# A fused attention and mixture-of-experts block: first norm transposed earlier, last gating ahead, residual biases spread over the kernel

## The reference, cut to what matters

```python
x = x + tanh(g_xattn[0]) * xattn(layernorm(x), ctx, ctx)            # 16 heads of 8
x = x + tanh(g_ffn[0]) * ffn(layernorm(x), ...)

def ffn(x, ...):
    attn_out = causal_attention(rope(x), rope(x), x) @ out_proj_w.T + out_proj_b
    x1 = layer_norm(x + attn_out, ln1_w, ln1_b)
    gates = softmax(x1 @ gate_w.T + gate_b)
    _, top_idx = top_k(gates, 2)
    expert_outputs = einsum('bsd,efd->bsef', x1, expert_w) + expert_b
    moe_out = (the two chosen experts' outputs, each times its gate, summed)
    return layer_norm(x1 + moe_out, ln2_w, ln2_b)
```

## Time and profile before

| | us |
|---|---|
| median of 3 runs | 441.61 |
| the profiled execution | 441.23 |
| its span, first to last instruction | 439.4 |
| PE busy | 385.7 (88%) |
| DVE busy | 369.2 (84%) |
| POOL busy | 323.3 (74%) |
| ACT busy | 288.4 (66%) |

### The profile page before, as it was taken

The page is one execution under the profiler, slowest core; times in us unless marked ns, Lnnn a source line. Parts: engine busy times, 40 slices in busy tenths (PEclk is TensorE's granted clock), DMA queues, the critical chain, the costliest instruction groups (busy, mean ns, idle before and its releaser), DMA issues.

```text
span 439.4 us, 17671 instructions
## 1 busy us (share of the span) xinstructions
PE 385.7 (88%) x6538; PEld 231.3 (53%) x6538; DVE 369.2 (84%) x1188; ACT 288.4 (66%) x728; POOL 323.3 (74%) x740
## 2 busy tenths in 40 slices
PE   0368888888888899999999999999999999999994
PEld 0134544454444555666666666666655555555541
DVE  6587999999997878888878878877848999999987
ACT  1126777767766766666666666666665788788772
POOL 4456767767778988888888788849823788888884
PEclk9999999999999999999999999999999999999999
DMA  6855686685553333333434343333000000000001
GB/s 163 193 155 160 170 199 169 162 180 145 132 158 101 98 100 105 104 106 104 109 106 125 103 127 100 99 105 96 12 4 2 1 25 13 24 27 12 25 25 48
DMA packets 88037, 42.76 MB, mean 97 GB/s; under 512 B 16000, under 2 KB 87824, under 8 KB 87952
## 3 DMA queue, kind: packets, MB, share of 16 engines
q1 hardware_dynamic: 80864, 39.59, 34.2%
q10 hardware_dynamic: 7088, 2.04, 2.0%
HBM read 5.69 MB, written 2.10 MB: 18 GB/s over the span
## 4 chain that ended last, share of the span: by engine, by line
PE 41%; DVE 6%; ACT 5%; issue 3%; POOL 1%; SPq 1%; DMA 1%; POOLq 0%; ACTq 0%; DVEq 0%
PE s_bank L923 6%; PE u_bank L499 6%; PE st_bank L923 6%; PE s_bank L421 4%; PE s_bank L434 3%; DVE r L697 2%; PE t_bank L413 2%; PE u_bank L944 2%; PE u_bank L942 2%; PE u_bank L909 2%; PE t_bank L407 2%; ACT z_x_t L1018 2%; ACT part L577 1%; PE u_bank L514 1%; PE t_bank L408 1%
## 5 line engine op out<-in xcount | busy, mean ns | idle before, releaser
L716 DVE TENSOR_REDUCE nm<-s_bank 128x4 f32<-128x512 f32 x256 | 171.5, 683 | 36.3 <-PE s_bank L434 34.0
L599 ACT ACTIVATE pt<-st_bank 128x512 f32<-128x512 f32 x250 | 147.5, 602 | 74.0 <-PE st_bank L434 51.6
L434 PE MATMUL s_bank<-qk 64*64 64x128 bf16 (+1 forms) x1584 | 103.5, 220 | 12.1 <-DVE nm L716 5.7
L499 PE MATMUL u_bank<-pt,vaug 128*32 128x128 f32 x2048 | 108.3, 286 | 1.6 <-DVE ao L733 0.2
L434 PE MATMUL st_bank<-qk 64*64 64x128 bf16 (+1 forms) x1540 | 98.2, 218 | 0.0
L434 PEld LDWEIGHTS s_bank<-qk 64*64 64x64 bf16 (+1 forms) x1584 | 73.8, 104 | 36.1 <-issue 18.9
L434 PEld LDWEIGHTS st_bank<-qk 64*64 64x64 bf16 (+1 forms) x1540 | 69.1, 103 | 0.0
L499 PEld LDWEIGHTS u_bank<-pt,vaug 128*32 128x32 f32 x2048 | 41.1, 108 | 27.5 <-issue 5.2
L421 PE MATMUL s_bank<-mqk,idb 64*64 64x256 bf16 x256 | 38.3, 292 | 0.8 <-ACT pt L599 0.4
L327 POOL TENSOR_TENSOR part<-r,part 128x512 bf16<-128x512 f32 x32 | 37.1, 1158 | 1.4
L421 PE MATMUL st_bank<-mkq,idb 64*64 64x256 bf16 x244 | 35.7, 293 | 0.0
(11 more groups left out here) (136 smaller groups left out, 815.4 us busy)
## 6 DMA issues: line engine op xcount, KB each, us to landing
qk<-part SPq DMA_DIRECT2D x221, 128.0 KB, 2.8
x_all<-x SPq DMA_DIRECT2D x16, 128.0 KB, 2.6
qk<-qrow SPq DMA_DIRECT2D x32, 64.0 KB, 2.0
c_all<-ctx_in SPq DMA_DIRECT2D x14, 128.0 KB, 2.8
out<-z_o SPq DMA_DIRECT2D x14, 128.0 KB, 1.8
qk<-mts ACTq DMA_DIRECT2D x34, 32.0 KB, 2.7
qk<-mts SPq DMA_DIRECT2D x30, 32.0 KB, 2.1
ewt<-exp_t SPq DMA_DIRECT2D x1, 512.0 KB
```

What stands on the lines that cost most here:

```text
L434: ins = pe.matmul(to[outs, :], fixed[:, outs], moving, start=not masked, stop=True, skip_group_check=masked)
L499: ins = pe.matmul(u_bank[b][32 * j:32 * j + 32, r * P:(r + 1) * P], v, pt[m % 4][:, j, :], start=half == 0, stop=half == 1, skip_group_che ...
L599: act.activation(pt[m % 4][:, :, :].rearrange("k j q -> k (j q)"), transposed_bank(m)[:, :], ACT.Exp).then_inc(ex, 1)
L716: dve.tensor_reduce(nm[q % 2][:, first:first + HEADS], s_bank[n % 2][:, :].rearrange("q (j k) -> q j k", j=HEADS), AX_X, ALU.max, negate=T ...
```

## The change

On PE, gated_sum is split: its first product is now sum_of_biases. The order of a full body becomes: experts 4 to 7, transpose of the attention, bias product, transpose of the first norm, gated sum, transpose of the gates, projection, logits, experts 0 to 3. In the body c = 16 the transposes of norm and gates come before the bias product. On ACT, the copy of the norm moves ahead of the second normalisation and of the copy of the gates. The exponentials of the last group's gates go between the two halves of the gating of group 14. On DVE the last group's shift of the logits is issued in body 16 behind the weighing of group 14, and its gating in body 17 ahead of the pair sum of group 14. On POOL the sixteen additions of the bias to the residual are issued one at step 0 of slots 19 to 28 (steps 152, 160, ... 224), one each in steps 242 and 246, and two each at the end of bodies 3 and 4; the two multiplications by tanh(g_ffn) are issued in step 144.

```diff
--- before.py
+++ after.py
@@ -931,7 +931,7 @@
                     pe.wait_ge(norm, SEQS - 1)
                 pe.transpose(u_bank[0][0:G * NE, W:W + P], zg[i][:, :, :].rearrange("q b e -> q (b e)"), idf[:, :]).then_inc(z_gt, 1)
 
-            def gated_sum(g, gc):
+            def sum_of_biases(g, gc):
                 i = gc % 2
                 pe.wait_ge(z_gtc, g + 1)
                 if gc == 0:
@@ -940,6 +940,9 @@
                     pe.wait_ge(z_all, (g - 1) * ALL + 1)
                 dst = u_bank[1][:, 0:W]
                 pe.matmul(dst, zgt[i][:, :], ebs[:, :], start=True, stop=False)
+
+            def gated_sum(g, gc):
+                dst = u_bank[1][:, 0:W]
                 pe.wait_ge(z_yq, g + 1)
                 pe.matmul(dst.rearrange("q (b d) -> q b d", b=G), idf[:, :], zyq[:, :, :],
                           start=False, stop=True).then_inc(z_yb, 1)
@@ -959,14 +962,21 @@
                     experts(s - 2, c - 2, 1)
                 if in_z(c, 0):
                     transpose_att(s, c)
+                if s - 1 == LAST:
+                    transpose_n(s - 1, c - 1)
+                    gates_t(s - 2, c - 2)
+                if in_z(c, 3) and s - 3 < LAST:
+                    sum_of_biases(s - 3, c - 3)
+                if in_z(c, 1) and s - 1 < LAST:
+                    transpose_n(s - 1, c - 1)
+                if s - 2 == LAST:
+                    gates_t(s - 2, c - 2)
                 if in_z(c, 3) and s - 3 < LAST:
                     gated_sum(s - 3, c - 3)
-                if in_z(c, 2):
+                if in_z(c, 2) and s - 2 < LAST - 1:
                     gates_t(s - 2, c - 2)
-                    if s - 2 == LAST:
-                        last_gated_sum(s - 2, c - 2)
-                if in_z(c, 1):
-                    transpose_n(s - 1, c - 1)
+                if s - 2 == LAST:
+                    last_gated_sum(s - 2, c - 2)
                 if in_z(c, 0):
                     project(s, c)
                 if in_z(c, 1):
@@ -1055,6 +1065,8 @@
                 if gc >= 1:
                     act.wait_ge(z_yp, g)
                 for b in range(G):
+                    if b == 1 and g == LAST - 1:
+                        gates_exp(LAST, gc + 1)
                     for e in range(HALF):
                         ins = act.activation(zyg[:, b, e, :], e_bank[b][1][:, e * P:(e + 1) * P], ACT.Copy,
                                              scale=zg[i][:, b, HALF + e:HALF + e + 1])
@@ -1072,22 +1084,25 @@
                     ins.then_inc(z_yg, 1)
 
             def body(s, c):
-                if in_z(c, 2):
+                if in_z(c, 2) and s - 2 < LAST:
                     gates_exp(s - 2, c - 2)
                 if in_z(c, 1):
                     normalise1(s - 1, c - 1)
                 if in_z(c, 0):
                     copy_att(s, c)
+                if in_z(c, 1):
+                    copy_x1(s - 1, c - 1)
+                if s - 1 == LAST:
+                    copy_gates(s - 2, c - 2)
                 if in_z(c, 4) and s - 4 < LAST - 1:
                     normalise2(s - 4, c - 4)
                 if s - 2 == LAST:
                     gate_last_experts(s - 2, c - 2)
-                if in_z(c, 2):
+                if in_z(c, 2) and s - 1 != LAST:
                     copy_gates(s - 2, c - 2)
-                if in_z(c, 1):
-                    copy_x1(s - 1, c - 1)
                 if in_z(c, 2) and s - 2 < LAST:
                     gate_experts(s - 2, c - 2)
+
             def early(n):
                 if n == DRAIN - 9:
                     copy_att(0, 0)
@@ -1260,14 +1275,19 @@
                                              in1=one(x_all, g * G + b), op0=ALU.mult, op1=ALU.add).then_inc(z_yo, 1)
 
             def body(s, c):
-                if in_z(c, 2):
+                if in_z(c, 2) and s - 2 < LAST:
                     shift_logits(s - 2, c - 2)
-                if in_z(c, 3) and s - 3 < LAST:
+                    if in_z(c, 3):
+                        gated_pairs(s - 3, c - 3)
+                    gating(s - 2, c - 2, (s - 3, c - 3) if in_z(c, 3) else None)
+                if s - 2 == LAST:
+                    gating(s - 2, c - 2)
                     gated_pairs(s - 3, c - 3)
-                if in_z(c, 2):
-                    gating(s - 2, c - 2, (s - 3, c - 3) if s - 3 < LAST else None)
+                    gated_sum(s - 3, c - 3)
                 if in_z(c, 2):
                     experts(s - 2, c - 2)
+                if s - 1 == LAST:
+                    shift_logits(s - 1, c - 1)
                 if in_z(c, 0):
                     attention_add(s, c)
                     experts_add(s - 3, c - 3)
@@ -1307,6 +1327,12 @@
             return early, steps
 
         def z_pool(pool):
+            FIRST_BIAS = (GROUPS + 3) * TILES
+
+            def last_bias(g):
+                pool.tensor_tensor(zpair(x_all, g), zpair(x_all, g), l2b[:, :].unsqueeze(1).broadcast_to([P, G, P]),
+                                   ALU.add).then_inc(z_xb, 1)
+
             def x1(g, gc):
                 i = gc % 2
                 pool.wait_ge(z_n, (g + 1) * G)
@@ -1366,16 +1392,20 @@
                     factor1(s, c)
                 if in_z(c, 3) and s - 3 < LAST:
                     factor2(s - 3, c - 3)
+                if c == 3 or c == 4:
+                    last_bias(2 * c + 6)
+                    last_bias(2 * c + 7)
 
             def early(n):
-                if n == DRAIN - 18:
+                if n == FIRST_BIAS - TILES:
                     for t in (l2w, l2b):
                         pool.tensor_scalar(t[:, :], t[:, :], tg[:, 1:2], 0.0, ALU.mult, ALU.add).then_inc(c_l2, 1)
                     pool.wait_ge(c_l2, 2)
-                g = n - DRAIN + 17
-                if 0 <= g < GROUPS:
-                    pool.tensor_tensor(zpair(x_all, g), zpair(x_all, g), l2b[:, :].unsqueeze(1).broadcast_to([P, G, P]),
-                                       ALU.add).then_inc(z_xb, 1)
+                g, t = divmod(n - FIRST_BIAS, TILES)
+                if 0 <= g < 10 and t == 0:
+                    last_bias(g)
+                if g == 11 and t in (2, 6):
+                    last_bias(10 + t // 4)
                 if n == DRAIN - 4:
                     factor1(0, 0)
                 if n == DRAIN - 2:
```

## The result

The changed kernel takes 445.77 us (median of 5 runs, 445.70 to 446.64), the kernel before, in the same comparison, 441.42 us (5 runs, 440.91 to 442.03). The ratio is 1.0102, with a 95% interval of 1.0087 to 1.0116: slower by about 1%. The profiled execution took 445.77 us, its span 444.0 against 439.4, at a granted clock of 0.997.

What follows compares the result with a forecast made beforehand. PE sets the pace (19.38 of 20 us busy, period 6.61 us), DVE close behind. 4.8 - 1.05 - 0.4 + 0.1 = +3.4 us on the profiled 441.23 gave 444.7, plus 0.38 for the median 445.0; range 443.2 to 447.0.

Steps and rivals of the forecast that it cites:

- Part 1's cycle: Full bodies, last stage: normalisation and gates' copy delay the logits, period 6.61 to 6.97 us plus 0.05 stalls, +4.8 us total.
- Rival A: Full bodies: the wait on the gates' copy never ends last, PE's 0.21 us idle goes, 437.5 us; chance 0.10.
- Rival C: Causal steps: a bias ahead of L284 makes POOL hold DVE, +2 us over ten steps, 447.0 us; chance 0.06.
- the two multiplications of step 144: POOL, causal steps: the two factors' scaling taken as hidden because POOL is often idle, bound 0 to 0.3 us.
- Nothing else catches it: Full bodies: no slack absorbs the lengthened cycle of +0.36 us a stage, summed through PE and ACT.
- Part 3's biases in the bodies: POOL, stages 3 and 4: four biases make only stage 5's first factor late, +0.1 us (0 to 0.5).
- the pair of normalisations: Drain: without a bias beside it, DVE's first pair ends 0.41 us sooner and PE gains that, -0.4 us (0 to -0.5).
- Part 3 as a whole: Biases out of the drain: -0.4 us in the drain, 0 in the causal steps, +0.1 in stages 3 and 4.
- Part 2: Tail: last group's gating issued earlier, so the last weighing starts sooner, -1.05 us (-0.4 to -1.6).
- the last gated sum on PE is ready about 0.5 us before DVE asks for it: Tail: PE's last gated sum would be ready about 0.5 us before DVE needs it.
- Rival D: Tail: ACT's longer queue eats the gain from earlier gating, +1.05, 446.0 us; chance included in the forecast's 0.80.
- The 0.38 us that the forecast added for the median: Whole kernel: the median of runs lies 0.38 us above the profiled execution, raising 444.7 to 445.0 us.

Runs made afterwards that it cites:

- Run 8: Changed kernel with bodies 3 to 15 back in the old order on PE and ACT, last stages and biases as changed: 441.38 us, ratio 1.0007.
- run 4: Changed kernel with one more ACT activation (0.39 us, output unused) ahead of the second normalisation in bodies 4 to 15: 453.38 us, ratio 1.0298.
- run 2: Kernel before with PE's new order alone in bodies 3 to 15, ACT's order kept: 442.83 us, ratio 1.0046.
- run 3: Kernel before with ACT's new order alone in bodies 3 to 15, PE's order kept: 459.0 us, ratio 1.04.
- run 5: Changed kernel with ACT's second normalisation ahead of the norm's copy and the gates' copy in bodies 4 to 15: 447.33 us, ratio 1.0143.
- run 12: Changed kernel, second normalisation before norm's copy, four biases in drain, DVE waiting for POOL and pausing 0.11 us before pair sum: 441.22 us, ratio 1.0.
- run 6: Changed kernel with the sixteen biases back in the drain and the factors' scaling back in step 239: 445.62 us, ratio 1.0108.
- run 7: Changed kernel with bodies 16 to 18 in the old order on all three engines, the rest as changed: 446.35 us, ratio 1.0118.
- run 9: Changed kernel with bodies 3 to 15 in the old PE and ACT order and the last four biases moved to the drain: 440.19 us, ratio 0.9971.

## Why the prediction held, and which of its terms were off

**Part 1's cycle: right.** The forecast named the wait (gates' copy, L1059, about 0.6 us), ACT's idle stretch ahead of the transpose, and 6.97 us a period plus 0.05 of stalls. Measured are 6.99 or 7.00, with 0.67. Run 8 puts the whole slowdown on this part, run 4 shows the normalisation on the cycle one to one, runs 2 and 3 that the ACT order is the costly half. Rival A, that the gates' copy never ends last, is refuted by the twelve waits. Rival C is refuted as well: with a bias ahead of L284 in ten steps, DVE and PE are no later behind the tenth than behind the first. In three of the ten traces DVE's L684 did take 0.48 us instead of 0.34 once, 0.04 us behind the start of L284, and the step was no longer for it. What did cost something there are the two multiplications of step 144, 0.19 us; the prediction took them as hidden, with a bound of 0.3.

**"Nothing else catches it": incomplete.** The prediction summed the cycle through PE and ACT only. A second chain lies close behind it: DVE's statistics, POOL's power and offsets, ACT's first normalisation, the attention's copy. In body 4 it decides, by 0.55 us over 7.00, since DVE's pair sum came 0.05 us ahead of the power. I had rows in which DVE and POOL hold each other up, applied them to the drain and to the causal steps, and not to the last stage, though body 3 of the kernel before shows it there (1.06 us at 334.73). The Trainium skill has the rule for exactly this pair, in "SBUF — State Buffer", section "SBUF: two separate sides": a DVE operation with two inputs in SBUF excludes a GpSimd operation that reads SBUF, and whichever starts first holds the port for its whole instruction. Runs 5 and 12 agree with it where POOL is the second (1.19 us instead of 0.70). They do not where DVE is: in run 12 the pair sum starts 0.20 us into a power and still takes 0.69 us, as alone. By the rule it would have to wait, so here the measurement decides. Rows 8 are finer than I read them, too: taken one by one, the first normalisation of the pair started 0.53 us into a bias and took the usual 0.34, and only the second, begun at 315.51, 0.11 us into the next bias, took 0.75.

**Part 3's biases in the bodies: mis-sized.** Forecast at +0.1 with a bound of 0.5, they cost 0.51 us in the changed kernel and 1.28 in run 8. The mechanism, a late first factor, was named; the slack of ACT behind it, on which I counted, is not there, as ACT's normalisation waited 1.92 us for the offsets. Without a bias beside it the pair of normalisations gives 0.40 us, as forecast (-0.4). The two multiplications take back 0.19. Part 3 as a whole thus costs 0.3 us (0.51 + 0.19 - 0.40), too little for the medians of run 6 and the changed kernel to show.

**Part 2: mis-sized, -0.84 by the traces and -0.6 by run 7, for -1.05.** The last weighing starts 1.72 us earlier relative to the logits of group 14 (430.08 to 433.80, with 5.44 at the logits), more than the forecast 1.05. But "the last gated sum on PE is ready about 0.5 us before DVE asks for it" failed: DVE waits 0.66 for it. ACT's second normalisation, which waits 1.70 us for POOL's offsets, stands ahead of the gating of the last experts. That gating starts at 434.83, 4.80 us later than the 430.03 of before, so 0.64 us earlier relative to the logits. PE's last sum starts 0.74 us behind it (0.77 before), its weight loads wait three times for it, and DVE waits for that sum. Up to DVE's last closing operation (436.28 to 440.73) the change still wins 0.99 us, close to the forecast; 0.15 is lost between it and the end of the span. Rival D is half true, by ACT's queue, as it said.

The sum forecast was 4.8 - 1.05 - 0.4 + 0.1 = 3.4 us; measured are 4.75 - 0.07 for part 1's cycle, 0.55 for the pair sum, 0.51 for the biases in the bodies, 0.19 for the two multiplications, -0.40 for the drain and -0.84 for part 2, 4.7 in all, and -0.09 of difference between the two executions gives 4.6. The forecast of 445.0 is 0.8 below the median. The misses, 0.55 for the pair sum, 0.4 for the biases, 0.2 for the multiplications and 0.2 for the last gating, have one sign and come from waits on POOL that I took for slack. The 0.38 us that the forecast added for the median hid a part of them, as the profiled execution and the median are both 445.77.

## What to carry to other kernels

When an operation is moved ahead on an in-order engine, sum the cycle again through everything that now stands between it and the next wait of the bounding engine. Here an idle stretch that a normalisation had filled for nothing became idle, and the normalisation moved onto the cycle. Then look for the second chain within a few tenths of the first, above all one that runs through two engines that can hold each other up. There 0.05 us of start order decided 0.5 us, and a pause of 0.11 us a body on the busy engine won 3.5 us net, which brought that order back to the time of the kernel before (441.22) and not below it. The gain that is left to take is run 9's: the old order of the full bodies, with the new tail and the biases moved to where POOL stood idle.

## What the runs showed of the hardware

A two-element operation is not cheap beside a wide one of the other engine. POOL's power takes 0.70 us alone or first, 1.01 to 1.24 if it starts during DVE's 128x512 pair sum, and then ends 0.55 to 0.57 us after that sum's end (run 5: 384.30 to 384.86). The starts say the same: the offsets behind the power begin 1.29 us after it in body 4 of the changed kernel, 0.80 in run 12. A wide operation of POOL holds DVE as well: in run 8 DVE's sum, begun 0.12 us into POOL's 128x256 addition (which ended at 354.88), took 1.15 us instead of 0.69 and ended 0.55 after it. The power does not. In the last stage of all fourteen traces the sum takes 0.68 to 0.71 us wherever a power starts within 0.7 us of it, and that holds where the power started first, by 0.02 to 0.68 us. So, of the two orders, power first costs neither engine anything, and sum first costs POOL 0.3 to 0.5 us.

A start late in the other's operation was harmless here: DVE's 128x128 row took 0.34 us when it began 0.6 us into POOL's 0.80, and 0.48 when it began 0.04 us into it (192.07 in the changed kernel's trace).

In run 3, PE idles 1.22 us ahead of the logits of each body of 7.58, and in some bodies the granted clock fell. The stretches of its profile, columns as in the earlier trace rows:

```profile
350.00:353.00 3.00, 2.95 (x15) 1.71 (x13) 2.66 (x12) 1.01 (x3) 2.82 (x6) 1.00 0.00 0
353.00:356.00 3.00, 1.83 (x6) 1.27 (x7) 2.13 (x12) 3.00 (x13) 1.87 (x5) 0.77 0.15 44
356.00:360.00 4.00, 4.00 (x9) 1.53 (x7) 3.54 (x19) 1.28 (x5) 3.66 (x9) 0.74 0.00 0
360.00:364.00 4.00, 2.78 (x18) 2.01 (x17) 2.36 (x13) 2.57 (x9) 1.39 (x2) 1.00 0.11 33
```

The four matmuls at 354.60 ran at the lower level, 1.2 GHz (3.66 us against 1.96), right behind the 1.22 us of idle time; 0.77 and 0.74 are means over stretches with both levels in them. Before and after that the clock is at 2.4 GHz. In the changed kernel, with 0.67 us idle ahead of the logits, it stays at 1.00 between 360 and 400 us. A shorter idle time is no safeguard, though: in run 5, with 0.60 us ahead of the logits of every second body, one group took 3.62 us (at 389.50, behind such a wait), in run 4, with 1.06, one took 3.50. Why these bodies and not the others was not settled.
